# A graph-attention kernel on one core: order of transfers, signals and adds in the six fill steps before its main loop

## The reference

```python
h = relu(layernorm(x))
x1 = x + elu(softmax(mask(leaky(f1 + f2))) @ h)      # f1, f2: two dots of each row of h
y = relu(layernorm(x1))
for l in range(3):                                   # the layers
    agg = softmax(mask(leaky(si + sj + b[l]))) @ y   # si, sj: two dots of each row of y
    z = layernorm(y + agg) * g1[l] + beta1[l]
    v = z + gelu(z @ W1[l] + b1[l]) @ W2[l] + b2[l]
    y = layernorm(v) * g2[l] + beta2[l]
out = x1 + y
```

## Time and profile before

| | |
|---|---|
| median of 3 runs | 2773.87 us (2773.44 to 2774.45) |
| the profiled execution | 2771.33 us |
| its span | 2769.5 us |
| first matmul of `hidden(0)` in step 0 | 108.36 us |
| pitch of a step: first ones, main loop, last layer | some 30.7, 27.4 and 26.25 us |
| mean granted clock of TensorE | 0.985 |

### The profile page before, as it was taken

The page is one execution under the profiler, slowest core; times in us unless marked ns, Lnnn a source line. Parts: engine busy times, 40 slices in busy tenths (PEclk is TensorE's granted clock), DMA queues, the critical chain, the costliest instruction groups (busy, mean ns, idle before and its releaser), DMA issues.

```text
span 2769.5 us, 53308 instructions
## 1 busy us (share of the span) xinstructions
PE 2651.5 (96%) x16771; PEld 2386.7 (86%) x16868; DVE 2138.1 (77%) x7995; ACT 2200.2 (79%) x4494; POOL 1689.8 (61%) x2197
## 2 busy tenths in 40 slices
PE   3699999999999999999999999999999999999997
PEld 2488888988888989888888888889888998998997
DVE  5898878777878777878777878777878777676674
ACT  4699888888888888888887888888878777777774
POOL 4467666566766565566676666555677554454655
PEclk8699999999999999999999999999999999999999
DMA  5221322222222221122222122222222211111111
GB/s 177 90 70 62 95 81 92 66 79 76 87 81 77 66 71 62 64 70 88 85 90 69 65 67 76 69 68 68 80 89 91 62 45 52 35 52 52 51 64 54
DMA packets 118589, 203.43 MB, mean 73 GB/s; under 512 B 12800, under 2 KB 85536, under 8 KB 118304
## 3 DMA queue, kind: packets, MB, share of 16 engines
q1 hardware_dynamic: 118304, 199.97, 22.3%
HBM read 116.05 MB, written 83.89 MB: 72 GB/s over the span
## 4 chain that ended last, share of the span: by engine, by line
PE 71%; DVE 12%; POOL 8%; issue 5%; ACT 3%; DMA 0%; DVEq 0%; SPq 0%; POOLq 0%; ACTq 0%
PE bank L605 32%; PE bank L588 26%; PE ps_u L564 7%; POOL xo L374 3%; DVE g_lo L983 3%; DVE st L957 2%; PE ps_u L646 2%; POOL rs L1283 2%; DVE ub L1074 2%; PE ps_s L559 2%; PE ps_s L551 1%; POOL hb L374 1%; DVE vb L952 1%; DVE ub L952 1%; ACT g_hi L859 1%
## 5 line engine op out<-in xcount | busy, mean ns | idle before, releaser
L605 PE MATMUL bank<-w_hi,g_hi 128*128 128x256 f32 x3072 | 890.5, 290 | 15.3 <-DVE g_lo L983 15.1
L605 PE MATMUL bank<-w_hi,g_lo 128*128 128x256 f32 x3072 | 865.2, 282 | 0.0
L605 PE MATMUL bank<-w_lo,g_hi 128*128 128x256 f32 x3072 | 863.9, 281 | 0.0
L859 ACT ACTIVATE g_hi<-bank,b_eff 128x512 fp32r<-128x512 f32 x768 | 529.3, 689 | 334.4 <-PE bank L588 327.9
L983 DVE TENSOR_TENSOR g_lo<-bank,g_hi 128x512 fp32r<-128x512 f32 x768 | 518.9, 686 | 202.3 <-ACT bank L861 188.2
L588 PE MATMUL bank<-zt_hi,w_hi 128*128 128x512 f32 x1536 | 632.4, 412 | 12.0 <-DVE g_lo L983 5.6
L588 PE MATMUL bank<-zt_hi,w_lo 128*128 128x512 f32 x1536 | 607.7, 396 | 0.0
L588 PE MATMUL bank<-zt_lo,w_hi 128*128 128x512 f32 x1536 | 606.4, 395 | 0.0
L605 PEld LDWEIGHTS bank<-w_hi,g_hi 128*128 128x128 f32 x3072 | 578.9, 188 | 24.2 <-DVE g_lo L983 23.1
L605 PEld LDWEIGHTS bank<-w_lo,g_hi 128*128 128x128 f32 x3072 | 579.2, 189 | 0.8
L605 PEld LDWEIGHTS bank<-w_hi,g_lo 128*128 128x128 f32 x3072 | 578.7, 188 | 0.0
(11 more groups left out here) (95 smaller groups left out, 4145.8 us busy)
## 6 DMA issues: line engine op xcount, KB each, us to landing
xb<-x_scratch SPq DMA_DIRECT2D x88, 512.0 KB, 4.0
x_scratch<-xo SPq DMA_DIRECT2D x64, 512.0 KB, 4.8
xin<-in_x SPq DMA_DIRECT2D x38, 512.0 KB, 5.9
r_scratch<-elu_r SPq DMA_DIRECT2D x32, 512.0 KB, 3.0
xin<-r_scratch SPq DMA_DIRECT2D x32, 512.0 KB, 4.6
out<-xo SPq DMA_DIRECT2D x32, 512.0 KB, 3.4
m<-m_scratch SPq DMA_DIRECT2D x96, 128.0 KB, 3.8
x_scratch<-h SPq DMA_DIRECT2D x24, 512.0 KB, 2.9
```

The source lines that it names most:

```text
L605: mm = pe.matmul(y, g[:, c, r * P:(r + 1) * P], w[:, l, c, :], start=(c == 0 and n == 0), stop=(c == C - 1 and n == 2))
L859: act.activation(g_hi[:, c, :], block_in, ACT.Gelu, bias=bias).then_inc(g_hi_ready, 1)
```

## The change

- SP: the load of x for group v0 stands ahead of the store of r.
- `h0_ready` counts one for each graph (four for a group) instead of one for a group. In the steps before 0 `row_dots` waits for each graph by itself; everything else waits for all four.
- In the steps before 0 the sum with x is one VectorE operation (128x1024) behind `elu_sums`, in place of four GpSimd operations. From step 0 on GpSimd does it as before.
- VectorE's list before step 0: the statistics of x first; `input_shift` behind `first_lows`; `made_variance` and `made_shift` next; `first_dots` ahead of `low_rows`; `mask_sums` ahead of `elu_sums`; both inverses at the end.
- ScalarE's list before step 0: `first_rows`, `high_rows`, `make_rows` and `elus` ahead of both exps.
- GpSimd's list before step 0: `input_root` ahead of `first_root`, and `residual_sum` is gone.

```diff
--- before.py
+++ after.py
@@ -437,16 +437,16 @@
             def body(st):
                 s = st.s
                 v0, v1, v2, v3 = early(s), middle(s), late(s), end(s)
+                if v0 and not ahead(v0) and v0 not in (1, 2):
+                    sp.wait_ge(h0_ready, st.nth0(v0 - 2 if v0 in (3, 4) else v0 - 1, T))
+                    sp.dma_start(x_rows(v0)[:, :, :], pick(x_u, st, v0)).then_inc(
+                        x_odd_in if v0 == 3 else xin_in, 32 if v0 == 4 else 16)
+                if v0 == 1:
+                    sp.wait_ge(h0_ready, st.nth0(0, T))
+                    sp.dma_start(x_rows(2)[:, :, :], pick(x_u, st, 2)).then_inc(xin_in, 32)
                 if v3 is not None and v3 < CH:
                     sp.wait_ge(x1_ready, st.nth0(v3))
                     sp.dma_start(pick(r_u, st, v3), elu_r[:, :, :]).then_inc(r_out, 16)
-                if v0 and not ahead(v0) and v0 not in (1, 2):
-                    sp.wait_ge(h0_ready, st.nth0(v0 - 2 if v0 in (3, 4) else v0 - 1))
-                    sp.dma_start(x_rows(v0)[:, :, :], pick(x_u, st, v0)).then_inc(
-                        x_odd_in if v0 == 3 else xin_in, 32 if v0 == 4 else 16)
-                if v0 == 1:
-                    sp.wait_ge(h0_ready, st.nth0(0))
-                    sp.dma_start(x_rows(2)[:, :, :], pick(x_u, st, 2)).then_inc(xin_in, 32)
                 if v2 is not None and v2 < CH:
                     if v2:
                         sp.wait_ge(x1_ready, st.nth0(v2 - 1))
@@ -789,7 +789,10 @@
                             act.wait_ge(agg0_done, st.nth0(v0 - 2, T))
                         if v0 >= CH + 2:
                             act.wait_ge(h_out, 16 * st.nth0(v0 - 2 - CH))
-                        normed(h0[v0 % 2], x_rows(v0), rs4, nm4, ACT.Relu).then_inc(h0_ready, 1)
+                        rows, h = x_rows(v0), h0[v0 % 2]
+                        for t in range(T):
+                            act.activation(h[:, t, :], rows[:, t, :], ACT.Relu, bias=nm4[:, t:t + 1],
+                                           scale=rs4[:, t:t + 1]).then_inc(h0_ready, 1)
 
                 def second_norm():
                     if live(s - 1):
@@ -839,12 +842,12 @@
                     next_above()
                     first_above()
                     first_norm()
+                    first_rows()
+                    high_rows()
+                    make_rows()
+                    elus()
                     next_exps()
                     first_exps()
-                    high_rows()
-                    first_rows()
-                    make_rows()
-                    elus()
                     turned()
                     if s == -4:
                         high_halves(0)
@@ -942,11 +945,13 @@
                 dve.wait_ge(e_done, nth(u))
                 dve.reciprocal(inv[:, :], sums[:, :]).then_inc(ready, 1)
 
-            def row_dots(nth, u, dot, rows, vec, ready, junk, graphs=range(T)):
+            def row_dots(nth, u, dot, rows, vec, ready, junk, graphs=range(T), made=None):
 
 
                 for t in graphs:
                     for j in range(2):
+                        if made is not None and j == 0:
+                            dve.wait_ge(made, nth(u, T, t + 1))
                         if t:
                             dve.wait_ge(ready, nth(u, 2 * T, 2 * t + j - 1))
                         dve.tensor_tensor_reduce(junk[:, j, :], rows[:, t, :], vec(j), 1.0, 0.0,
@@ -1015,10 +1020,12 @@
 
                 def first_dots():
                     if v0 is not None:
-                        dve.wait_ge(h0_ready, st.nth0(v0))
+                        if s >= 0:
+                            dve.wait_ge(h0_ready, st.nth0(v0, T))
                         if live(s + 3) and s >= 0:
                             dve.wait_ge(dots_ready, st.nth(s + 3, 2 * T))
-                        row_dots(st.nth0, v0, dots0, h0[v0 % 2], lambda j: v_row[:, j, :], dots0_ready, junk)
+                        row_dots(st.nth0, v0, dots0, h0[v0 % 2], lambda j: v_row[:, j, :], dots0_ready, junk,
+                                 made=h0_ready if s < 0 else None)
 
                 def sum_rows():
                     if live(s + 1):
@@ -1133,6 +1140,11 @@
                             ins = dve.scalar_tensor_tensor(out=rows, in0=ps_u[r][:, :], scalar=1.0, in1=rows,
                                                            op0=ALU.min, op1=ALU.add)
                         ins.then_inc(elu_sum, 1)
+                        if s < 0:
+                            dve.wait_ge(elu_sum, st.nth0(v2))
+                            dve.wait_ge(xr_in, 16 * st.nth0(v2))
+                            dve.tensor_tensor(elu_r[:, :, :], elu_r[:, :, :], residual_x(v2)[:, :, :],
+                                              ALU.add).then_inc(x1_ready, 1)
 
                 def second_statistics():
                     if live(s - 1):
@@ -1146,26 +1158,26 @@
                         variance(st.nth, s - 1, mv2, ve2, mv2_ready, ve2_ready)
 
                 if s < 0:
+                    input_statistics()
+                    input_variance()
                     sum_rows()
                     first_variance()
                     next_lows()
                     first_norm()
                     first_lows()
-                    input_statistics()
-                    input_variance()
+                    input_shift()
                     made_variance()
-                    input_shift()
-                    next_inverses()
-                    first_inverses()
                     made_shift()
+                    first_dots()
                     low_rows()
-                    first_dots()
-                    elu_sums()
                     next_dots(range(T))
                     first_heads()
                     next_heads()
                     if sums_early:
                         mask_sums(v0)
+                    elu_sums()
+                    next_inverses()
+                    first_inverses()
                     if s == -4:
                         low_halves(0)
                     return
@@ -1356,12 +1368,11 @@
 
                 if s < 0:
                     mask()
+                    input_root()
                     first_root()
-                    input_root()
                     made_root()
                     first_mask()
                     scaled_rows()
-                    residual_sum()
                     if s == -4:
                         low_halves(0)
                     return
```

## The result

The changed kernel takes 2756.16 us (median of 4 runs, 2755.30 to 2756.83) beside 2773.65 for the kernel before in the same comparison: ratio 0.9938 (95% interval 0.9921 to 0.9955), 17.5 us by the medians. The two profiled executions, 2771.33 and 2756.02, differ by 15.3. Forecast were a gain of 16.1 us and a time of 2757.8.

What follows compares the result with a forecast made beforehand. TensorE, 96% busy, lacked work only before the main loop, so step 0's start bounds. Walking steps -6 to -1 moved `hidden(1)` from 124.36 to 108.3, 16.1 us: 2773.87 - 16.1 = 2757.8 us, range 2753 to 2764.

Steps and rivals of the forecast that it cites:

- The bound and the place: Missing TensorE work lies in the first two slices of 69 us, ahead of the main loop; step 0's start decides.
- The walk: Forecast of new times for steps -6 to -1 up to step 0's entry, giving a gain of 16.1 us.
- The aggregate to `hidden(1)`: Entry to step 0 on PE: aggregate starts at 106 (122.00 before), `hidden(1)` at 108.3 (124.36 before).
- Company: Step -4: GpSimd's eight low halves, 5.50 us alone, run beside VectorE's work and end at 47.75, a loss of 2.75.
- GpSimd is not late: Rival, 16%: in step -4 low halves slip between VectorE operations or `adj` lands earlier; gain 19, time 2755.
- Transfers bind: Rival, 15%: before step 0 VectorE waits for loads of x, step -2's 3 us late; gain 11.5, time 2762.
- Part is given back after step 0: Rival, 6%: something other than PE, perhaps a transfer, holds steps 0 to 3; half the gain goes, 2766.
- Slower by 96 signals: Rival, 3%: per-graph signals of h in all 32 groups, 96 more, cost time; at 0.3 us each, 2786.
- The text's own test: Sign of being wrong: a gap of over 2 us between the shift of `hidden(1)` and that of the end.

Runs made afterwards that it cites:

- the run without company: Changed kernel, but GpSimd's low halves wait until VectorE's low halves are done, place and order kept: 2757.57 us, ratio 0.9945 to the kernel before.
- The run with `adj` ahead: Changed kernel with the attention rows issued behind `adj` of group 2, GpSimd's low halves in their old place: 2754.03 us, ratio 0.9931 to the kernel before.
- the low halves split: Changed kernel with GpSimd's low halves cut in two, four operations each in steps -3 and -2 behind input_root: 2753.74 us, ratio 0.9930 to the kernel before.

## Why the prediction was right, and where not

**The bound and the place: right.** All that changed lies before step 0. `hidden(1)` was named as what the sum must move; it moved by 16.6 us (16.1 forecast), and `row_turns` of step 0 by 16.6.

**The walk: right within half a microsecond at most places.** Forecast and measured: dots of group 0 at 13.52, 13.60; their head at 16.41, 16.49; h(1) 20.77, 20.90; head(1) 24.3, 24.73; turned weights 26.0, 25.56; head(2) 33.6, 33.91; `adj` landed 37.15, 37.13 (issued 3.3 us earlier and landed 1.5 earlier, so it did stand in the line of the weights, which moved by 1.4); low halves' end 47.75, 47.92; `input_shift(3)` 51.05, 51.22; x added(1) 63.45, 63.96; (2) 80.3, 80.7; norm 89.2, 89.46; `turns(1)` 100.9, 101.28; `hidden(0)` 102.0, 102.05; `next_scores` 104.75, 104.56; aggregate 106, 106.17.

**Terms that were off.** (1) "So mask sum to 37.85, ELU sums to 39.05, x added at 40.35": the mask sum started at 37.68, 0.55 us after `adj` had landed. The trace ends its wait with the store of an older mask, `m_scratch<-m_new`, which SP issued right behind `adj`. In each of nine profiles VectorE's mask sum starts 0.37 to 0.49 us after GpSimd's first operation on the same `adj`; whether the store follows `adj` in line or the hand-over takes that long isn't told apart. Beside GpSimd's mask and low halves the mask sum took 0.92 and the sum with x 1.44, so x was added at 41.2. (2) The sum with x: 1.22 taken, 1.23 measured in three steps and 1.44 beside the low halves, well inside the ends 1.1 and 1.7. (3) The aggregate to `hidden(1)`: the walk kept the 2.3 us of the earlier trace rows. It took 1.61 us. Before, the granted clock was 0.50 to 122 us, 0.59 from 122 to 124 and 1.00 from 124 on, so the aggregate ran in part at the lower level; PE had been idle for 9.41 us ahead of `next_scores`. Now PE works from 101.28 on with one gap of 0.79 us, and the clock is 0.92 from 104 to 106 and 1.00 from 106 on. These 0.75 us are what makes 16.6 out of 16.1 at `hidden(1)`; the rest of the walk was 0.2 short.

**Company.** "Three get through by 44.3, five more take 3.45: 47.75, a loss of 2.75": 8.45 us against 5.52 alone, so 2.9. This was the term with the least behind it, and the run without company settles it. Advanced Engine Details and Errata (VectorE Performance Modes) of the Trainium skill has GpSimd and VectorE block each other where VectorE runs in a two-port mode; it doesn't say so of operations with two SBUF inputs, as the prediction reads it. Here both lose (3.32 against 2.45, 8.45 against 5.52), but less than by strict turns: the times alone add up to 9.2 us (5.52, 2.45, 1.22) where the whole took 8.45. For VectorE's dots the pace stayed 0.865 us from start to start (99.43, 100.29, 101.16), below the 1.04 that full blocking would make.

**The rivals.** *GpSimd is not late* didn't come: low halves were late by what was said. The run with `adj` ahead shows in part what it would have given: without the sum with x in company, and with most of VectorE's first low half over, the eight lose 1.1 us in place of 2.9. *Transfers bind* didn't come: no load of x is named in VectorE's waits up to 112 us, and the statistics of group 4 start at 64.05, right behind the sum. The kernel with SP's order undone shows what a late load costs: VectorE waits 5.75 and 4.52 us there. How near the loads of the changed kernel came isn't shown. *Part is given back after step 0* came, by 1.2 us and in step 2, but not by a transfer: by PE's clock. (Step 2 took 32.3 us before, not the 30.7 that the rival gives to all.) The text's own test, a gap of over 2 us between the two shifts, was not met. *Slower by 96 signals*: `hidden(1)` and the pitch of steps 0, 1 and of all from 3 on are as they were, so 96 signals cost nothing that can be seen.

**Against the median.** The shift at the end, 15.3 us, is that of two profiled executions; by medians the gain is 17.5 us. The kernel before ran 64 times in all comparisons, from 2771.33 to 2776.54 us, with no gap between two groups. 39 of these runs took over 2773 us, and both profiled ones (2771.33, 2772.27) are among the 25 below. That the longer runs lose their clock in step 2, as the changed kernel does, would account for most of the 2.2 us between the two gains. The mean granted clock leans that way (0.9850 over 23 of the runs below 2773 us, 0.9844 over 36 above), but it doesn't say where the clock fell. No profile shows such a run, so it stays open. The forecast of 2757.8 took one shift, 16.1 us, from the profile's and from the median's time alike. The one is 15.3 and the other 17.5, so that 2756.16 came out within 1.7 us is in part luck.

**What the parts are worth.** Undone one at a time at `hidden(1)`: SP's order 12.1 us, the three lists 8.5 (ScalarE's alone 4.4), the sum on VectorE 4.5, signals a graph 2.1. Less what `adj`'s landing did in these executions (1.7 and 1.5), SP's order, the lists, the sum and the signals still add up to 24 where the whole gives 16.6, and SP's order alone gives 0.9. (1.45 of the lists' 8.5 and 1.6 of ScalarE's 4.4 are the clock's.) The parts are no addends: they are links of one chain.

## What to carry to other kernels

Putting a load ahead pays only where nothing else holds the engine that uses it: here the same move is worth 0.4 us or 10. So walk the chain with each engine's list, and take parts away from the whole as well as adding them to the old kernel. Where VectorE works on two SBUF inputs beside GpSimd, price both at the pace in company, and put the longer work where its engine waits anyway. When the fill of a pipeline is shortened, look for the transfer that all of it hangs on (here `adj` of one step) and issue it ahead of what is not due yet.

## What the runs showed of the chip that was not expected

- The granted clock fell to 0.50 in step 2 in both profiles of the changed kernel and in seven of its variants (pitches of 33.5 to 33.8 us). It stayed at 1.00 with the low halves split and with those without company (32.32 and 32.33), in both profiles of the kernel before and in that with SP's order alone. PE's work around it is the same in all, down to a stretch of 2 us in which it is busy for 0.6. What decides is not in these runs. It costs 1.2 to 1.5 us.
- Ahead of step 0 the clock is part of what a wait costs. The aggregate took 3.19 us with the clock at 0.50, 2.36 in the kernel before, and 1.61 where PE had begun 2.9 us earlier than in the first. So 0.75 of the 16.6 us gained at `hidden(1)` are clock.
- How long `adj` takes to land differs from one execution to the next: 9.5 to 11.2 us in six profiles with the same transfers ahead of it, issued at 27.3 to 27.6, and 9.52 and 9.66 in the two of the changed kernel itself. SP's next issue, the mask to `m_scratch`, took 2.3 to 2.95 us in them, where most of its issues take 0.4 to 0.5. Since the chain runs through `adj`, this goes into the time one to one.
